# A mixture-of-experts tail on one core: the last expert tile's addition and the addition ahead of it

## The reference, cut to what matters

```
gate_out = einsum('bsd,ed->bse', x, Wg)           # 8 experts
top_v, top_i = top_k(gate_out, 2)                 # each row goes to 2 different experts
probs = softmax(top_v)
for e in range(8):
    w_e = sum(probs * (top_i == e), axis=-1)
    g = silu(x @ W1[e].T) * (x @ W2[e].T)         # 512 wide
    out = out + (g @ W3[e].T) * w_e[..., None]
x = x + tanh(g_ffn[0]) * out
```

## Time and profile before

| | |
|---|---|
| median of 3 runs | 621.73 us (621.47 to 621.78) |
| the profiled execution | 621.88 us |
| its span | 620.1 us, granted TensorE clock 0.995 |
| busy: PE, DVE, POOL, ACT | 588.6, 404.3, 309.0, 272.3 us |
| instructions | 10909 |
| `out_dram<-yg,ids` additions | 36 |

### The profile page before, as it was taken

How to read it: one execution, slowest core, us unless ns; L and a number is a source line. 1 busy time by engine, 2 the same in 40 slices (tenths; PEclk the granted TensorE clock), 3 DMA queues, 4 the chain that set the end, 5 groups by cost and what they waited for, 6 DMA issues and landing times.

```text
span 620.1 us, 10909 instructions
## 1 busy us (share of the span) xinstructions
PE 588.6 (95%) x2882; PEld 342.4 (55%) x2883; DVE 404.3 (65%) x1266; ACT 272.3 (44%) x713; POOL 309.0 (50%) x272
## 2 busy tenths in 40 slices
PE   4899999999999999999999999999999999999992
PEld 2444465555546555556555565556665666566661
DVE  3578978898997989988899986266352332223220
ACT  2765665556555655655656564222322112211220
POOL 3643554565564698564796564512573222222221
PEclk9999999999999999999999999999999999999997
DMA  8944576587776789777688676999676443333321
GB/s 317 328 112 105 117 157 166 126 182 151 164 161 163 172 186 212 146 157 191 145 206 179 145 168 141 287 332 297 135 156 122 67 60 53 49 42 49 53 27 22
DMA packets 113971, 93.74 MB, mean 151 GB/s; under 512 B 38512, under 2 KB 107504, under 8 KB 113904
## 3 DMA queue, kind: packets, MB, share of 16 engines
q1 hardware_dynamic: 91824, 70.37, 46.9%
q10 hardware_dynamic: 15360, 13.64, 10.0%
q0 software_dynamic: 6720, 8.95, 8.8%
HBM read 27.72 MB, written 12.36 MB: 65 GB/s over the span
## 4 chain that ended last, share of the span: by engine, by line
PE 71%; DVE 14%; issue 5%; DMA 5%; ACT 4%; ACTq 1%; POOL 0%; SPq 0%; POOLq 0%; DVEq 0%
PE ps_s L1648 17%; PE ps_o L1467 13%; PE ps_s L1419 9%; PE ps_o L1676 8%; PE ps_a L1477 6%; DVE blocksT L1144 5%; DVE probs L1132 4%; DMA out_dram<-yg,ids 4%; PE ps_t L1359 4%; PE ps_o L1432 2%; PE ps_t L1669 2%; ACT probs L732 2%; PE ps_a L1359 2%; PE ps_t L1419 2%; PE ps_t L1352 1%
## 5 line engine op out<-in xcount | busy, mean ns | idle before, releaser
L603 POOL TENSOR_TENSOR probs<-probs,inv_sum 128x802 f32<-128x802 f32 x128 | 195.3, 1526 | 138.2 <-DVE inv_sum L1121 137.1
L732 ACT ACTIVATE probs<-probs,neg_max 128x401 f32<-128x401 f32 x256 | 159.3, 624 | 106.5 <-DVE neg_max L1132 99.0
L1648 PE MATMUL ps_s<-w_sb,xgT 128*128 x288 | 135.4, 593 | 1.5 <-DVE xgT L1150 1.5
L1132 DVE CUSTOM_DVE_ANT_0 probs<-ps_s,biases 128x401 f32<-128x401 f32 x215 | 116.1, 571 | 21.7 <-PE ps_s L1419 20.6
L1144 DVE STREAM_TRANSPOSE blocksT<-probs 128x832 f32<-128x832 f32 x124 | 129.0, 1040 | 0.3 <-POOL probs L603 0.3
L650 POOL DMA_INDIRECT out_dram<-yg,ids x36 | 56.1, 1558 | 144.2 <-DVE yg L1301 107.6
L1467 PE MATMUL ps_o<-probsT,v_sb 128*64 128x512 f32 x496 | 113.3, 598 | 0.0
L1419 PE MATMUL ps_s<-kT,qT 64*128 64x201 f32 (+1 forms) x860 | 108.2, 346 | 3.5 <-DVE neg_max L1132 2.8
L1419 PEld LDWEIGHTS ps_s<-kT,qT 64*128 64x128 f32 x860 | 83.8, 186 | 44.1 <-issue 27.2
L866 ACT COPY gatedT<-ps_t 128x512 f32<-128x512 f32 x36 | 21.1, 586 | 150.8 <-PE ps_t L1669 146.3
L1291 DVE TENSOR_TENSOR gated<-ps_s,silu 128x512 f32<-128x512 f32 x36 | 24.9, 691 | 94.3 <-PE ps_s L1648 82.0
(11 more groups left out here) (172 smaller groups left out, 515.2 us busy)
## 6 DMA issues: line engine op xcount, KB each, us to landing
probsT<-blocksT SPq DMA_DIRECT2D x276, 96.0 KB
probsT<-blocksT SPq DMA_DIRECT2D x92, 128.0 KB
probsT<-blocksT ACTq DMA_DIRECT2D x96, 96.0 KB
xg_blocks<-x_regrouped SPq DMA_DIRECT2D x156, 32.0 KB
probsT<-blocksT ACTq DMA_DIRECT2D x32, 128.0 KB
w_sb<-W1T_dram SPq DMA_DIRECT2D x8, 512.0 KB, 5.1
w_sb<-W2T_dram SPq DMA_DIRECT2D x8, 512.0 KB, 6.0
w_sb<-W3T_dram SPq DMA_DIRECT2D x8, 512.0 KB, 7.2
```

The source lines that it names most:

```text
L603: pool.tensor_tensor(duo, duo, inv_sum[:, u:u + 2].unsqueeze(2).to_broadcast([P, 2, LASTK]), ALU.mult)\
L732: act.activation(probs[:, b, 0:LASTK], probs[:, b, 0:LASTK], ACT.Exp, bias=neg_max[:, b:b + 1], scale=-1.0, accum_out=sum_exp[:, b:b + 1]) ...
L1132: dve.tensor_tensor_reduce(probs[:, b, 0:LASTK], scores_bank(u)[:, 0:LASTK], biases[:, tile, :], HD ** -0.5, 3e38, ALU.add, ALU.min, neg_m ...
L1648: mm = pe.matmul(bank[:, :], xgT[:, buf, k, :], w_sb[:, bass.ds(expert, 1), (n * KT + k) * FH:(n * KT + k + 1) * FH].squeeze(1), start=(k ...
```

## The change

The last tile's addition gets a semaphore of its own, `last_added`, and waits for `added` to reach a number that POOL reads from a third entry of `n_tiles`. DVE works that number out in four more steps of the third phase, which has 26 steps now: step 22 marks the experts whose running count is one less than that of all, step 23 takes the largest mark (1 when the phase's last tile is the first one of its expert, 0 otherwise), step 24 adds the phase's count and N1 - 2 = 14, and step 25 multiplies by 16. With T tiles in all the number is 16(T - 2) where the tile ahead is of the same expert, and 16(T - 1) where it is of another. The four steps stand at tile 8 of the DVE program, ahead of the table writes and of the two semaphores. SP waits for `last_added` at the very end, after its loop over s, and in the loop for one addition fewer.

```
-SCHED_TILES = {2: (1, range(0, 12)), 3: (1, range(12, 24)), 7: (2, range(0, 11)), 8: (2, range(11, 22))}
+SCHED_TILES = {2: (1, range(0, 12)), 3: (1, range(12, 24)), 7: (2, range(0, 11)), 8: (2, range(11, 26))}
...
-        n_tiles = sb("n_tiles", [1, 2], I32)
+        n_tiles = sb("n_tiles", [1, 3], I32)
...
-        ids_ready, added = sem("ids_ready"), sem("added")
+        ids_ready, added, last_added = sem("ids_ready"), sem("added"), sem("last_added")
...
-            sp.wait_ge(added, 16 * FULL)
+            sp.wait_ge(added, 16 * (FULL - 1))
             for s in range(FULL, NG):
                 sp.wait_ge(xg_in[s % RING], 16 * 5 * (s // RING + 1))
                 with sp.If(there > s):
-                    sp.wait_ge(added, 16 * (s + 1))
+                    sp.wait_ge(added, 16 * s)
+            sp.wait_ge(last_added, 16)
...
-                def add_rows(s, slot, buf):
+                def add_rows(s, slot, buf, ahead=None, done=added):
                     pool.wait_ge(y_ready, s + 2)
                     pool.wait_ge(ids_ready, s + 1)
-                    if not first(s, 1):
+                    if ahead is not None:
+                        pool.wait_ge(added, ahead)
+                    elif not first(s, 1):
                         pool.wait_ge(added, 16 * s)
                     if not isinstance(s, int):
                         pool.sem_inc(carried, 1)
                     pool.indirect_dma_start(out=out, out_offset=bass.IndirectOffsetOnAxis(ap=ids[:, slot:slot + 1], axis=0),
-                                            in_=yg[:, buf, :], in_offset=None, compute_op=ALU.add).then_inc(added, 16)
+                                            in_=yg[:, buf, :], in_offset=None, compute_op=ALU.add).then_inc(done, 16)
...
-                add_rows(last_tile(pool), RING, 2)
+                ahead = pool.value_load(n_tiles[0:1, 2:3], min_val=16 * (FULL - 2), max_val=16 * (NG - 1))
+                add_rows(last_tile(pool), RING, 2, ahead, last_added)
...
-                count = 22 if last else SCHED_OPS
+                count = 26 if last else SCHED_OPS
...
                     if n == 22:
-                        ins = dve.tensor_tensor(used[:, :], used[:, :], here, ALU.add)
+
+                        ins = dve.tensor_scalar(sums[:, 1, :], ends, ends[:, NE - 1:], -1.0, ALU.subtract, ALU.is_equal) \
+                            if last else dve.tensor_tensor(used[:, :], used[:, :], here, ALU.add)
                     if n == 23:
-                        ins = dve.tensor_scalar(used_rows[:, :], used[:, :], float(P), None, ALU.mult)
+                        ins = dve.tensor_reduce(sums[:, 2, 0:1], sums[:, 1, :], AX.X, ALU.max) if last else \
+                            dve.tensor_scalar(used_rows[:, :], used[:, :], float(P), None, ALU.mult)
+                    if n == 24:
+
+                        ins = dve.scalar_tensor_tensor(out=sums[:, 2, 1:2], in0=ends[:, NE - 1:], scalar=float(N1 - 2),
+                                                       in1=sums[:, 2, 0:1], op0=ALU.add, op1=ALU.add)
+                    if n == 25:
+                        ins = dve.tensor_scalar(n_tiles[:, 2:3], sums[:, 2, 1:2], 16.0, None, ALU.mult)
                     ins.then_inc(route, 1)
```

## The result

| | before | with the change |
|---|---|---|
| median, 22 runs of each | 622.17 us (621.47 to 623.15) | 620.87 us (620.31 to 621.48) |
| span of the profiled execution | 620.1 us | 619.1 us |

The ratio is 0.9979, with a 95% interval of 0.9973 to 0.9985: 1.3 us faster (0.9 to 1.7), where 1.9 had been forecast. The forecast time was 619.8 in a range of 619.1 to 621.0; it started from 621.73, and over 22 runs before stands 0.44 us higher, which is a part of the distance. The case that was forecast without any rival reached only to 620.1; the measured time lies in the part of the range that half of rival A had added.

A forecast was written before the change was run, and what follows sets the result against it. PE is busy 588.6 of 620.1 us, but the end hangs on POOL's last addition and closing DRAIN. The start's -1.89 us, with 0 for the rest, takes the median from 621.73 to 619.8, range 619.1 to 621.0.

The forecast's parts named there:

- The case that was forecast without any rival: Kernel's end: 0.28 to 0.78 us of issue and a landing of 3.76 to 3.95 give 619.1 to 620.1 us; chance 0.77.
- rival A: Last addition: code loading as PE and DVE leave delays its landing, giving back 1.83 us (621.6; half, 620.7); chance 0.12.
- The wait goes in full: Last addition: it waits only for tiles 0 to 33, landed over 5 us before yg, so yg is next to be late.
- The other bound, 0.28: Last addition's start: 0.28 us after yg, as for the addition ahead, giving 610.2; 0.78 us after L649 was taken instead.
- The steps, the second load and SP: Tile 8's gate slips 0.65 to 0.85 us, POOL's load hides by 2.2, SP's some 0.5 is worth nothing; cost 0.
- The start moves by 1.89 us: Last addition: its start moves from 612.72 to 610.83, by 1.89 us, at most by 2.5.
- I take 3.79: Last addition: it lands 3.79 us after its start, as before, at 614.6; bounds 3.76 and 5.62.
- 7.18 to the DRAIN's end: POOL's closing DRAIN: it ends 7.18 us after the last addition's start, at 618.0, and the span at 618.2.
- Rival B: Kernel's end: POOL's DRAIN is tied to something other than the last addition, so the time stays at 621.7; chance 0.04.
- C: POOL between yg and the last addition: a code-loading stall of 4.55 us, PE's price, makes it slower, 624.4; chance 0.05.
- D: Last tile: on the chip it opens its expert, so one wait stays as it was, 621.7; chance 0.02.
- A sign I had announced wrongly: Changed profile: the idle time before the last addition is put down to DVE's yg; still the DMA would mean D.

## Why the prediction was right, and where its size was off

**The wait goes in full: right.** The number that the schedule works out leaves the wait for tiles 0 to 33, and yg is what the last addition waits for. It starts 0.92 us behind yg; 0.93 had been forecast, from the 0.78 us of issue. The other bound, 0.28, is excluded in every run of the change.

**The steps, the second load and SP: right.** The gate slipped by 0.84 us (0.65 to 0.85 forecast) and PE's transposes not at all. SP's branches moved out of its tail without effect, until the DRAIN was gone.

**"The start moves by 1.89 us": the mis-sized term.** It was the difference to one execution, and in that execution the addition ahead took 5.62 us to land, the longest of the eleven profiles in which PE and DVE leave as usual. These have 5.62, 5.35, 4.74, 4.94, 5.22, 5.18, 5.47, 4.93, 5.02, 5.08 and 5.48 us, mean 5.18. A last addition that waits starts 0.81 us behind that, so on the mean 5.99 us after the one ahead; without the wait it was 4.5 in every run. That is 1.5 us, not 1.9. The step that was off is thus the length of the wait that the change takes away; that the wait goes, and goes in full, was right.

**"I take 3.79" for the landing, and 7.18 to the DRAIN's end: in part wrong.** Rival A was right in its mechanism and small in its effect. The last addition can be held up too: without the wait, and with PE and DVE leaving, it landed in 3.8 to 4.8 us, 4.3 on the mean of eight profiles. But POOL's own work in the DRAIN covers that up to a landing of about 4.3 us. Of the kernels without the wait and with the whole DRAIN only the first profile of the change went beyond, and lost 0.45 us. 1.5 us less 0 to 0.45 is 1.05 to 1.5, and 1.3 was measured; how often executions without a profile lose something isn't known. A had priced the delay as if the DRAIN followed the landing in full. The argument against it had taken the one late share for all there was, but further code packets come behind it. And the earlier trace rows were read as the late share moving: what moved from 609.89 to 610.84 was mostly the code packet, and the share's rest only followed. The time lies in the range only by the part that A had added: less the 0.44 us by which before stands higher it would be 620.43, still above the forecast case's 620.1. That the shorter wait and A's delay together stayed under 621.0 is partly luck.

**Rival B** is excluded: where the landing is in time, the DRAIN ends 7.18 us behind the start of the last addition, wherever that lies (seven profiles). What B warned of is true in part, since the end isn't tied to the start alone: with a landing at 4.8 us it was 7.63. **C** didn't occur: between yg and the addition there is no gap over 1 us in any run of the change. **D** is excluded by the start itself, since the addition ahead landed 0.9 us after it.

**A sign I had announced wrongly:** the idle time before the last addition was to be put down to yg. It is put down to the DMA in all runs, also where that DMA landed later. The landing that another engine sees decides, not the name in the bracket.

**A rule beside the rows.** The Trainium skill ("DMA: Bandwidth & Descriptors", Why a DMA increments its semaphore by 16 and not by 1) says that sixteen engines finish apart and each adds one. The trace agrees: before, fifteen increments of the addition ahead are in by 610.04 and the sixteenth comes at 611.92, and a whole wait hangs on it. Rival A had argued that a share which meets code is held no longer than a packet. That the share goes on as soon as the code packet ends agrees with it; the share was 1.88 us behind the other fifteen, though, and the 16 KB packet took 0.95 us.

What stays open: what holds back the last addition in each case, and whether DVE's leaving has a part in it. How the DRAIN's work is made up is a fit to a few DRAINs and one forecast that held; that it goes by the number of indirect DMAs, and not by something else that grows with them, wasn't tested.

## What to carry to other kernels

Before taking out a wait, ask why what it waits for is late: here the wait cost 0.05 us when PE and DVE stayed in their block, and 1.2 to 1.9 in the three profiles in which it stood and they left while the DMA was under way. A size read from one execution is a size of that execution; where one DMA share decides, several profiles are needed. And look at who leaves last: POOL's closing DRAIN was worth 2.7 us here, twice the change, and both without it and with a second one placed in idle time the kernel beat both versions (616.81 and 617.28 us beside 619.48 for the change and 620.63 for before).

## What the runs showed of the hardware that I had not expected

- POOL's DRAIN behind indirect DMAs fits work in proportion to how many have been issued since the last DRAIN: 5.64 us for 68 and 5.23 us for 63 (590.94, its end, less 585.71) make 0.083 us each, 2.04 us for 24 make 0.085. About half of it comes behind the last landing: 2.8 us for 68, 1.8 for 44, 0.9 for 20, 0.2 for 5. It took its full 5.7 us when all had landed before it started.
- Leaving its last block took PE 3.4 to 4.6 us, and it held back one share of the addition that was under way by 1.0 to 1.9 us (4.7 to 5.6 us to land, 3.7 to 3.8 when PE stayed). The rest of that share followed a 16 KB instruction packet of 0.95 to 1.56 us, and landed 1.01 to 1.08 us behind it in all eleven profiles.
- The granted clock fell to 0.50 (1.2 GHz) for 3.4 us in the same part of the attention in ten of fourteen executions, with PE busy in it. In the changed profile PE had been busy for the 2 us before (367 to 369), and the stretch took 1.4 us longer than in the profile of before, which has no dip.
